# One core, four layers: single blocks at the head of two norms, a last norm block by block, bias rows that open a sum, and gates moved into an earlier period

## The reference

```python
x = x + attn_a(layernorm(x))    # attention over channels, softmax(q^T k / 4)
x = x + ffn(layernorm(x))       # 6 routed experts with top-k weights, 2 shared
x = x + attn_b(layernorm(x))    # gated delta rule, 16 heads of 128, 4-tap convolution
x = x + ffn(layernorm(x))       # the same weights as the second layer
```

## Time and profile before

| | us |
|---|---|
| plain runs, median of three | 3394.36 |
| lowest and highest | 3393.52, 3399.66 |
| profiled execution, its own time | 3396.07 |
| span of that execution | 3394.3 |
| PE busy, VectorE busy, ScalarE busy | 3237.4, 2161.3, 1488.2 |

### The profile page before, as it was taken

One profiled execution on the slowest core, in us unless ns is written; L12 is line 12 of the kernel. 1 busy time (PEld: TensorE's weight loads), 2 busy tenths in 40 slices (PEclk: granted clock), 3 DMA queues, 4 the chain that ended last, 5 costly groups with the idle time before them and its releaser, 6 DMA issues. The chain is left out here.

```text
span 3394.3 us, 78389 instructions
## 1 busy us (share of the span) xinstructions
PE 3237.4 (95%) x33424; PEld 1532.6 (45%) x33424; DVE 2161.3 (64%) x3580; ACT 1488.2 (44%) x3420; POOL 125.9 (4%) x457
## 2 busy tenths in 40 slices
PE   8999999997889999999999999999999869999999
PEld 4444444443444444444444444444444434444443
DVE  2454425425789888888878888888898526451441
ACT  2221102204566765776676577567667533110110
POOL 0000000000000000000000000000000000000000
PEclk9999999998989999999999999999999779999999
DMA  3031322122101111121111211111211012222211
GB/s 121 0 90 60 88 78 65 47 74 88 40 30 42 36 61 37 33 76 46 39 52 44 66 33 52 43 40 42 67 43 36 12 70 91 66 87 76 61 56 68
DMA packets 97945, 191.53 MB, mean 56 GB/s; under 512 B 10184, under 2 KB 35400, under 8 KB 95296
## 3 DMA queue, kind: packets, MB, share of 16 engines
q1 hardware_dynamic: 97600, 186.51, 17.6%
HBM read 171.54 MB, written 14.94 MB: 55 GB/s over the span
## 5 line engine op out<-in xcount | busy, mean ns | idle before, releaser
L1734 PE MATMUL psum<-dl_xt,dl_wqkv 128*128 128x512 f32 x1536 | 761.7, 619 | 9.6 <-DVE dl_qkv L1373 9.6
L1373 DVE SCALAR_TENSOR_TENSOR dl_qkv<-psum,dl_par,dl_qkv 128x511 f32<-128x511 f32 (+2 forms) x576 | 428.9, 745 | 33.9 <-ACT dl_tails L1212 24.9
L521 PE MATMUL psum<-xnt_sb,wmats 128*128 128x512 f32 x896 | 408.9, 593 | 1.1 <-DVE f_partial L789 1.1
L1734 PEld LDWEIGHTS psum<-dl_xt,dl_wqkv 128*128 128x128 f32 x1536 | 262.4, 190 | 265.6 <-issue 229.8
L521 PE MATMUL psum<-f_token_sums,wmats 128*128 128x512 f32 x672 | 306.8, 592 | 0.0
L789 DVE TENSOR_TENSOR f_partial<-f_partial,psum 128x512 f32<-128x512 f32 x112 | 77.1, 688 | 311.2 <-PE psum L521 309.9
L521 PEld LDWEIGHTS psum<-xnt_sb,wmats 128*128 128x128 f32 x896 | 169.1, 190 | 214.1 <-issue 207.9
L1741 PE MATMUL psum<-dl_wo,dl_sg 128*128 128x512 f32 x512 | 256.7, 620 | 0.1
L672 ACT ACTIVATE f_partial<-psum 128x512 f32<-128x512 f32 x32 | 19.1, 597 | 510.5 <-PE psum L521 510.5
L1208 ACT ACTIVATE dl_qkv<-psum,dl_par 128x512 f32<-128x512 f32 x192 | 149.1, 776 | 197.8 <-PE psum L1734 197.8
L577 PE MATMUL psum<-f_wdown,f_hidden_b 128*128 128x512 f32 x512 | 221.7, 593 | 3.4 <-DVE x_sb L812 3.4
(11 more groups left out here) (232 smaller groups left out, 4738.0 us busy)
## 6 DMA issues: line engine op xcount, KB each, us to landing
dl_wqkv<-in_dw_qkv SPq DMA_DIRECT2D x192, 256.0 KB, 2.6
f_wdown<-in_wdowns SPq DMA_DIRECT2D x64, 512.0 KB, 3.6
wmats<-in_wmats SPq DMA_DIRECT2D x56, 512.0 KB, 3.5
dl_wo<-in_dwo SPq DMA_DIRECT2D x16, 1024.0 KB, 5.5
f_weights_b<-f_weights_by_expert SPq DMA_DIRECT2D x24, 512.0 KB, 9.1
x_sb<-in_x SPq DMA_DIRECT2D x4, 1024.0 KB, 9.1
x_after_experts<-x_sb SPq DMA_DIRECT2D x16, 256.0 KB, 2.6
dl_wfb<-in_dwfb SPq DMA_DIRECT2D x16, 256.0 KB, 3.4
```

Source lines behind the costliest of these rows:

```text
L521: ins = pe.matmul(ps[:, bank, :], wm[:, m % WRING, block, k, :], moving[:, k, :], start=(fresh and k == 0), stop=(last_of and k == 1), ski ...
L1373: tap_ = lambda dl: dve.scalar_tensor_tensor(y_[:, dl:TT], ps[:, bank, 0:TT - dl], par[:, h, 4 * a + 3 - dl:4 * a + 4 - dl], y_[:, dl:TT], ...
L1734: last = pe.matmul(ps[:, bank, :], wq[:, n % RING, m, :], xt[:, u // HG % 2, m, :], start=(m == 0), stop=(m == KC - 1))
```

## The change

The norms' groups now end at blocks 1, 2, 4, 8, 12 and 16, in place of 4, 8, 12 and 16; the loads of x follow them (six loads), and the constants are loaded behind the second. A group's next statistics and root stand behind its second block, or its only one. In the expert stages `bias(e)` for e = 1 to 3 opens the sum of its tile: it stands ahead of the tile's down products, each of its matmuls waits for the read of its bank, and the down products no longer wait. Bias(1) and bias(3) stand directly behind the tile before; bias(2) stands behind the products of group 1 of the second pair. The last down product of tiles 1 to 3 closes the sum and signals blocks one by one. VectorE's last tile in the first expert stage goes add, statistics, factors, normalise, one block behind the other, with ScalarE's roots to match. In the delta stage the four gates of unit 15 move from slots 2 and 3 of period 16 to slots 9 to 12 of period 15.

```diff
@@ norm_stage
-        size = 4 if meanvar is None else NT
-        groups = NT // size
+        ends = (1, 2, 4, 8, 12, 16) if meanvar is None else (NT,)
+        groups = len(ends)
+        bounds = [slice(a, b) for a, b in zip((0,) + ends[:-1], ends)]
+        x_in = [sem(tag + f"x_in{q}") for q in range(groups)]
...
-                    for q in range(4):
-                        sp.dma_start(x_sb[:, 4 * q:4 * q + 4, :], rows[:, 4 * q:4 * q + 4, :]).then_inc(x_in[q], 16)
-                        if q == 0 and constants_from is not None:
+                    for q, part in enumerate(bounds):
+                        sp.dma_start(x_sb[:, part, :], rows[:, part, :]).then_inc(x_in[q], 16)
+                        if q == 1 and constants_from is not None:
...
                         normalize(i)
-                        if i == size * q + 1 and q + 1 < groups:
+                        if i == min(bounds[q].start + 1, bounds[q].stop - 1) and q + 1 < groups:
                             statistics(q + 1)
...
-                    if i % size == 1 and i // size + 1 < groups:
-                        deviation(i // size + 1)
+                    if i == min(bounds[q].start + 1, bounds[q].stop - 1) and q + 1 < groups:
+                        deviation(q + 1)
+                    if i == bounds[q].stop - 1:
+                        q += 1
@@ ffn_stage, PE
-                            if g == 0 and c == 0 and q > 0:
-                                pe.wait_ge(acc_read, 4 * (2 * p + side - 1) + i + 1)
+                            ends = q >= GROUPS and g == GROUPS - 1 and c == HC - 1
                             last = pe.matmul(ps[:, 4 + i, :], hid[:, i * P:(i + 1) * P], wd[:, q % DRING, c, :],
-                                             start=(g == 0 and c == 0), stop=False)
+                                             start=(q == 0 and c == 0), stop=ends)
+                            if ends and i < 3:
+                                last.then_inc(acc_ps, 1)
...
-                        pe.matmul(ps[:, 4 + i, :], wt[rows, e, :], bd[rows, :], start=False, stop=True).then_inc(acc_ps, 1)
+                        if e > 0:
+                            pe.wait_ge(acc_read, 4 * (e - 1) + i + 1)
+                        ins = pe.matmul(ps[:, 4 + i, :], wt[rows, e, :], bd[rows, :], start=(e > 0), stop=(e == 0))
+                        if e == 0:
+                            ins.then_inc(acc_ps, 1)
...
+                        if p > 0 and g == 1:
+                            bias(2 * p)
                         down(p, 0, g - 1)
...
                     down(p, 0, GROUPS - 1)
-                    bias(2 * p)
+                    if p == 0:
+                        bias(0)
+                    bias(2 * p + 1)
...
-                    bias(2 * p + 1)
@@ ffn_stage, ACT
-                    for e in range(2, FN):
-                        deviation(4 * e, 4 * e + 4)
-                        for i in range(4 * e, 4 * e + 4):
-                            take_x(i)
+                    deviation(8, 12)
+                    for i in range(8, 12):
+                        take_x(i)
+                    deviation(12, 13)
+                    for i in range(13, NT):
+                        deviation(i, i + 1)
+                        take_x(i - 1)
+                    take_x(NT - 1)
@@ ffn_stage, DVE
+                def put_block(i):
+                    if i < 4:
+                        dve.wait_ge(acc_ps, i + 1)
+                    elif i % 4 < 3:
+                        dve.wait_ge(acc_ps, 4 + 3 * (i // 4 - 1) + i % 4 + 1)
+                    else:
+                        dve.wait_ge(down_done, GROUPS * (i // 4 + 1))
+                    dve.tensor_tensor(x_sb[:, i, :], ps[:, 4 + i % 4, :], x_sb[:, i, :], ALU.add).then_inc(acc_read, 1)
...
-                put_out(2 * PAIRS - 1)
-                if normed_to is not None:
-                    statistics(3)
-                    factors(3, 12, 16)
-                    for i in range(12, 16):
-                        normalize(i)
+                if normed_to is None:
+                    put_out(2 * PAIRS - 1)
+                else:
+                    for i in range(12, NT + 1):
+                        if i < NT:
+                            put_block(i)
+                            block_statistics(i)
+                        if i > 12:
+                            factors(i - 10, i - 1, i)
+                            normalize(i - 1)
@@ short_jobs
+    if k == UNITS:
+        table = {at: jobs for at, jobs in table.items() if jobs[0][0] != "gate"}
+    if k == UNITS - 1:
+        table |= {(9 + n, "inner"): [("gate", k, n, every)] for n in range(4)}
```

More of the change, by code:

```diff
@@ L140, in norm_stage @@
         bank_free = [sem(tag + f"bank_free{b}") for b in range(2)]
-        x_in = [sem(tag + f"x_in{q}") for q in range(4)]
         const_in = sem(tag + "const_in")
         stored = sem(tag + "stored")
-        size = 4 if meanvar is None else NT
-        groups = NT // size
+        ends = (1, 2, 4, 8, 12, 16) if meanvar is None else (NT,)
+        groups = len(ends)
+        bounds = [slice(a, b) for a, b in zip((0,) + ends[:-1], ends)]
+        x_in = [sem(tag + f"x_in{q}") for q in range(groups)]
         with nc.Block() as block:
@@ L172, in statistics @@
                             dve.wait_ge(x_in[q], 16)
-                        for i in range(size * q, size * q + size):
+                        for i in range(bounds[q].start, bounds[q].stop):
                             o.done(dve.bn_stats(st[:, i, :], x_sb[:, i, :]))
                         o.wait()
-                        for i in range(size * q, size * q + size):
+                        for i in range(bounds[q].start, bounds[q].stop):
                             last = dve.bn_aggr(mv[:, i, :], st[:, i, :])
@@ L180, in factors @@
                 def factors(q):
-                    part = slice(size * q, size * q + size)
+                    part = bounds[q]
                     dve.wait_ge(std_ready, q + 1)
@@ L211, in _ @@
                 deviation(0)
+                q = 0
                 for i in range(NT):
@@ L807, in hide, with block_statistics @@
                         dve.tensor_tensor(h, h, act_g[:, c, side], ALU.mult).then_inc(hidden, 1)
+                def put_block(i):
[6 more added lines that the diff above has]
+                    dve.tensor_tensor(x_sb[:, i, :], ps[:, 4 + i % 4, :], x_sb[:, i, :], ALU.add).then_inc(acc_read, 1)
                 def put_out(e):
                     for i in range(4 * e, 4 * e + 4):
-                        dve.wait_ge(acc_ps, i + 1)
-                        dve.tensor_tensor(x_sb[:, i, :], ps[:, 4 + i % 4, :], x_sb[:, i, :], ALU.add).then_inc(acc_read, 1)
+                        put_block(i)
                 def statistics(e):
                     for i in range(4 * e, 4 * e + 4):
-                        dve.wait_ge(acc_read, i + 1)
-                        step(dve.bn_stats(st[:, i, :], x_sb[:, i, :]))
-                        dve.bn_aggr(mv[:, i, :], st[:, i, :]).then_inc(var_ready, 1)
+                        block_statistics(i)
+                def block_statistics(i):
+                    dve.wait_ge(acc_read, i + 1)
+                    step(dve.bn_stats(st[:, i, :], x_sb[:, i, :]))
+                    dve.bn_aggr(mv[:, i, :], st[:, i, :]).then_inc(var_ready, 1)
                 def factors(n, first, end):
```

## The result

| | before | after |
|---|---|---|
| median of 14 plain runs, us | 3394.43 | 3401.97 |
| lowest and highest | 3392.49, 3399.66 | 3392.89, 3404.96 |
| span of the profiled execution | 3394.3 | 3398.8 |

After over before is 1.0017, with a 95% interval of 1.0009 to 1.0025. The forecast was 3393.2 with a range of 3386.5 to 3399.5: the kernel became 7.5 us slower, and the range was missed by 2.5.

The account below looks back on a forecast made before the run. TensorE, busy 95% of the span, was taken to bound the kernel. The terms 2.7 + 0.4 + 5.2 - 2.9 - 3.4 - 1.9 - 1.3 = -1.2 on 3394.36 gave 3393.2 us, range 3386.5 to 3399.5.

Parts of the forecast that it names:

- Resume at 3053.4: +2.7: Start of tile 1, expert stages: PE held until VectorE's fourth read and the last bias matmul, 2.7 us later than before.
- Norm one, +2.7: Norm one: head start of 3.7 us, 6.4 lost as blocks 1, 2 and 4 come late; net +2.7.
- I take +2.7, since the nearest rows after the start are all at the quick pace: Norm one: +2.7 chosen within bounds +2.1 and +6.7, the upper having PE slow again behind two gaps.
- rival 3: Norm one: PE is slow again behind the gaps, +4.0 us, giving 3397.2; chance 0.14.
- Bias rows, +2.6 a stage: Changes of tile in both expert stages: 7.5 us in place of 5.0 ahead of the tail, +5.2 in all.
- Rival 4: Tile 1: VectorE's reads don't hold PE, bias matmuls slip between passes; -2.7 us twice, 3387.8; chance 0.06.
- Tails: Ends of the expert stages: -2.9 us in the second, -3.4 in the first, as the last tile is read earlier.
- Gates, -1.9 and -1.3: Delta stage: period 15 saves 1.9 us as the clock holds through slot 12 and one more; tail saves 1.3.
- Rival 1: Period 15: the clock doesn't hold, +2.0 us in place of -1.9, giving 3397.1; chance 0.20.
- Norm four, +0.4: Norm four: head start wins 4.6 us, single blocks lose 5.1, net +0.4; bounds -0.6 and +1.5.

Follow-up runs that it names:

- tile1_closed: Changed kernel with bias(1) back closing tile 1, tiles 2 and 3 as changed: 3395.64 us, 0.9999 of the kernel before.
- norms_only: Kernel before with only the norms' groups ending at 1, 2, 4, 8, 12, 16: 3401.36 us, 1.0018 of the kernel before.
- tile1_wait: Changed kernel with bias(1) closing tile 1 and one wait for all four reads ahead of tile 1's first down product: 3396.89 us, 1.0009 of before.
- all_mended: Changed kernel with next root ahead of ScalarE's copy (groups ending at 1, 2, 4) and bias matmuls in the middle of every sum: 3382.54 us, 0.9962 of before.
- after_again: The changed kernel run once more with no edit: 3399.25 us, 1.0011 of the kernel before.
- mid_sum: Changed kernel with every tile's four bias matmuls together in the middle of its sum, down products opening and closing it: 3389.24 us, 0.9978 of before.
- tile1_filled: Changed kernel with three unused 128-row identity matmuls put between those of bias(1): 3415.07 us, 1.0063 of the kernel before.
- sums_only: Kernel before with only the expert stage's part: bias rows, closing passes, last tile block by block: 3400.99 us, 1.0017 of the kernel before.
- gates_only: Kernel before with only the last unit's gates moved into its own period: 3391.24 us, 0.9989 of the kernel before.
- root_ahead: Changed kernel with ScalarE taking the next root before its copy in groups ending at 1, 2, 4: 3392.55 us, 0.9989 of the kernel before.

## Why the prediction was wrong

The step that failed is in the sum of the bias rows: "Resume at 3053.4: +2.7" prices the start of tile 1 by PE's wait and its passes, and puts the clock behind them at nothing. The runs show 1.7 there in each expert stage, 3.4 in all, and with that one placement undone (tile1_closed), which takes away the clock's 1.7 and the 1.6 that was forecast for it in each stage, the loss can't be told from none. Two more clock terms, in norm one and at the start of attention, came on top.

*Norm one, +2.7: mechanism right, clock wrong.* The head start was 4.8 (forecast 3.7: the table load waited for block 0's statistics alone and came at 4.46; I had put it behind the constants, at 5.6; in three other profiles, norms_only, tile1_wait and all_mended, the root behind it waited 0.9 to 1.1 for the constants, so the head start of 4.8 is the better end), the loss behind three held-up roots 6.6 (6.4): +1.8 where no gram ran slowly. So in the execution that the sum is set against, the term was good to 0.9. Over all executions a step failed here too: "I take +2.7, since the nearest rows after the start are all at the quick pace". Those rows had no gap before them, so they said nothing of a matmul behind one. Seven profiles have these gaps. In four (norms_only and tile1_closed with two blocks each, after_again and tile1_wait with one) grams ran at 1.2 GHz; in the other three (after, mid_sum, tile1_filled) attention's first matmuls did. None escaped, and none had both. Kernels with the old norm one (before, sums_only, gates_only) have neither; of the two with the root ahead, which have no gaps, root_ahead has the slow attention and all_mended neither. A slow gram costs 1.5 to 1.7, a slow start of attention about 1.7 in passes (+1.9 in the stage). So rival 3, with a chance of 0.14, came true in four profiles of seven, at 1.5 to 3.2 in place of its 4.0, but not in the profile of after. There attention paid 1.9, for which the working had no term; that the gaps are the cause of that isn't shown.

*Bias rows, +2.6 a stage: the term was mis-sized.* From bias(0) to the down product was 4.74 where 4.7 was said, and bias(2), bias(3) and the end of tile 2 came as worked out. Missing is a term of 1.7: the first product of tile 1 at 1.2 GHz. The clock was weighed in norm one and in period 15, but not here, where the change replaces passes by short matmuls behind waits. The four profiles with bias rows at the head of tile 1 and no filler (after, after_again, sums_only, root_ahead) show the fall in both stages, eight of eight; before, norms_only, gates_only and tile1_closed have none in eight, and bias(3) at the head of tile 3, in 1.97 and behind one wait, goes without a fall in the same four profiles, eight of eight. tile1_closed shows that it is this placement; what in it the chip answers to stays open, since the wait alone (tile1_wait) gave one fall in two, and matmuls of 128 rows between the bias matmuls (tile1_filled) made the fall longer. Rival 4 (the reads don't hold PE) is refuted by [0.76 <-DVE] and 2.91 for four matmuls.

*Tails: right.* Second stage: the span's end came 3.2 closer to the last down pass (2.9 forecast). First stage 3.8 (3.4).

*Gates, -1.9 and -1.3: right in kind, and by luck in sum.* The slots gave -2.6: the clock held through slot 13, as forecast, and 1.4 us into slot 14, which took 3.90 in place of 4.48. The tail gave -0.6: its first product came 3.2 earlier (3.1), but the slow clock cost 2.6, not 1.8, since a pair of turns fell into it beside the four passes (1.91 in place of 1.04). Together -3.2, the forecast, by luck, as the two errors of 0.7 cancel; timed alone -4.0. Rival 1 is refuted.

*Norm four, +0.4: right.* It measured -0.4, within the bounds, because the first block landed in 2.6, the lower of my two ends.

*The rest.* The delta stage was to be 3.2 shorter and was 0.5 shorter: up to slot 9 of period 15, in code that wasn't touched, it took 2.7 us more than in the profile of before. Up to there the granted clock was 1.2 GHz for about 96 us in after and 81 us in before, which fits; why it fell oftener isn't shown. The stage took 2010.6 to 2014.7 in the three profiles with its old code and 2003.7 to 2014.8 in the nine with the gates moved, so 2.7 is within the scatter of executions. Set against the six stages, the miss of 5.7 in the spans is attention 1.9, experts 1.2 and 1.6, delta 2.7, less 0.9 and 0.8 for the norms. The plain runs lost 7.5, the profiled one 4.5. Norm one took 59.2 in this profile and up to 62.4 in the others, which would fit, and the delta stage scatters by as much; the plain runs have no trace, so that stays open.

The range was too narrow mainly because its clock terms were too few: norm one (up to 3.2), tile 1 (1.7 twice) and attention (1.9) all point the same way, and the last two weren't in it.

## What to carry to other kernels

Where a change puts a short wait or a string of small matmuls into a stream that runs at 2.4 GHz, give the clock a term of its own at that place, with a chance, and look for it in the next dense work behind as well, even over a stage's border. To let a sum be read early, let its last product close it block by block and put the small bias matmuls into the middle, where PE works without a break; ahead of the sum they stand between waits. When groups are made smaller to start sooner, move what the next group waits for ahead of the work of the present one on every engine's queue, not on the first alone: this one reorder on ScalarE was worth 6 us of norm one. It gave only 1.1 in norm four.

## What the runs showed of the hardware

- In after the granted clock fell about 5.0 us behind the end of tile 0's last down pass, for some 3.4 us, with bias(0), 0.76 of waiting and 2.9 of seven-row matmuls between. In root_ahead it fell once while bias(1) still ran (3.86 for its four matmuls) and stayed down 6.8 us. A plain wait of 2.65 in the same place was followed by a fall once of two.
- In tile1_filled, with identity matmuls of 128 rows and seven-row matmuls in turn, PE stayed at 1.2 GHz for over 13 us while busy without a gap, and came back some 6 us into the dense product behind them, in both stages.
- At the start of after the granted clock reads 1.00 while the first gram takes 4.61 in place of 2.32.
- A seven-row matmul over 512 columns alone takes 1.05 (two passes); four in four row groups together take 1.11, as the earlier trace rows have it.
